# Two-layer attention and feed-forward kernel on one core: banks of the last wide products, products without a reader in TensorE's waits, and an earlier load of the exponential's table

## The reference, cut to what matters

```python
x = x + xattn0(layernorm(x), ctx, ctx)      # 16 heads of 16, softmax attention, Wq Wk Wv Wo
x = x + ffn0(layernorm(x))                  # 256 -> 1024 -> 256: layernorm, 8-bit levels of the activations, ternary weights, exact gelu, layernorm, levels
x = x + xattn1(layernorm(x), ctx, ctx)      # 8 heads of 32, mLSTM form: see below
x = x + ffn1(layernorm(x))                  # base product plus gated low-rank part: see below

# xattn1, over sequences of 128 tokens
pre = 15 * tanh((concat(q, k, v) @ ifgate_w.T + b) / 15)
i_pre, f_pre = pre[..., :8], pre[..., 8:]
log_d = cumsum(log_sigmoid(f_pre)) differences + i_pre, causal;  m = rowmax(log_d)
h = (q k^T / sqrt(32) * exp(log_d - m)) v / (max(|row sum|, exp(-m)) + 5e-5)
out = h / rms(h) * (1 + outnorm_w)

# ffn1: 8 experts of rank 16
gate = softmax(xt @ gate_w.T)
out = xt @ weight.T + (1 / 16) * sum over e of gate_e * (xt @ U_e.T) @ V_e.T
```

## Time and profile before

| | us |
|---|---|
| median of three runs | 413.37 |
| the profiled execution | 413.97 |
| its span (first to last instruction) | 412.3 |
| TensorE busy | 334.4 (81%) |
| VectorE busy | 305.8 (74%) |
| ScalarE busy | 264.3 (64%) |
| gates: last gates' rows turned to first log_d | 289.2 to 297.6 |
| drain: end of the last values' product to the end | 386.3 to 412.3 |

### The profile page before, as it was taken

One profiled execution on the slowest core, in us unless ns is written; L12 is line 12 of the kernel. 1 busy time (PEld: TensorE's weight loads), 2 busy tenths in 40 slices (PEclk: granted clock), 3 DMA queues, 4 the chain that ended last, 5 costly groups with the idle time before them and its releaser, 6 DMA issues.

```text
span 412.3 us, 9147 instructions
## 1 busy us (share of the span) xinstructions
PE 334.4 (81%) x3086; PEld 236.6 (57%) x3093; DVE 305.8 (74%) x1025; ACT 264.3 (64%) x567; POOL 183.8 (45%) x207
## 2 busy tenths in 40 slices
PE   2989789998999999724667778779488999999774
PEld 1777567776777767402445545456265666666431
DVE  2799736877889888676998999984447877788641
ACT  1466445476455455626789889876578888888520
POOL 1213401122122564239998989962015455544520
PEclk9999999999999999955999999989689999999966
DMA  7799998979634510000000000000002122212000
GB/s 239 211 291 264 262 249 221 234 177 227 134 85 115 123 22 2 1 0 0 2 1 2 0 2 1 2 0 2 0 14 40 40 41 53 52 46 46 16 25 25
DMA packets 43869, 33.68 MB, mean 82 GB/s; under 512 B 19888, under 2 KB 39728, under 8 KB 43696
## 3 DMA queue, kind: packets, MB, share of 16 engines
q1 hardware_dynamic: 43824, 33.11, 32.7%
HBM read 24.71 MB, written 8.39 MB: 80 GB/s over the span
## 4 chain that ended last, share of the span: by engine, by line
PE 57%; DVE 18%; issue 13%; ACT 8%; POOL 3%; DMA 1%; SPq 0%; DVEq 0%; ACTq 0%; POOLq 0%
PE PS L1461 6%; PE PS L1157 5%; PE PS L1238 5%; PE PS L1227 4%; DVE sm L741 4%; PE PS L1296 4%; PE PS L1218 4%; PE PS L1217 4%; PE PS L1451 4%; PE PS L1257 3%; PE PS L1446 3%; PE PS L1424 3%; ACT pT L991 2%; DVE sm L713 2%; PE PS L1400 2%
## 5 line engine op out<-in xcount | busy, mean ns | idle before, releaser
L991 ACT ACTIVATE pT<-PS 128x512 f32<-128x512 f32 x64 | 36.5, 596 | 48.2 <-PE PS L1218 47.9
L606 DVE TENSOR_REDUCE negm<-PS 128x4 bf16<-128x512 f32 x64 | 42.3, 684 | 13.0 <-PE PS L1227 12.8
L435 POOL TENSOR_TENSOR sm<-sm,mhalf 128x1 f32<-128x1 f32 x16 | 11.3, 708 | 81.1 <-DVE sm L638 81.1
L451 POOL TENSOR_TENSOR kst<-kst,rows 128x1024 f32<-128x1024 f32 x16 | 37.7, 2354 | 6.4 <-ACT kst L1059 6.3
L1103 ACT ACTIVATE lnT<-PS,Atok 128x128 f32<-128x128 f32 x128 | 36.5, 369 | 4.3 <-PE PS L1402 2.7
L1336 PE MATMUL PS<-identf,w2f 128*128 128x128 f32 x128 | 19.2, 298 | 21.0 <-ACT w2f L1048 20.8
L1218 PE MATMUL PS<-identb,negm 128*128 128x128 bf16 x256 | 34.9, 220 | 0.0
L465 POOL TENSOR_TENSOR kst<-kst,rows 128x1024 f32<-128x1024 f32 x14 | 33.1, 2366 | 0.0
L1238 PE MATMUL PS<-pT,vx 128*32 128x128 f32 x512 | 27.0, 285 | 5.2 <-ACT pT L991 5.2
L1336 PEld LDWEIGHTS PS<-identf,w2f 128*128 128x128 f32 x128 | 15.1, 151 | 25.5 <-ACT w2f L1048 20.2
L1461 PE MATMUL PS<-wd,xT 128*128 128x392 f32 x64 | 28.0, 565 | 1.8 <-DVE rest L885 1.8
(11 more groups left out here) (220 smaller groups left out, 975.6 us busy)
## 6 DMA issues: line engine op xcount, KB each, us to landing
scr_q<-qpart SPq DMA_DIRECT2D x8, 384.0 KB, 3.4
scr_k<-kpart SPq DMA_DIRECT2D x8, 384.0 KB, 4.5
X<-in_x SPq DMA_DIRECT2D x8, 256.0 KB, 4.6
CTXT<-in_ctxT SPq DMA_DIRECT2D x8, 256.0 KB, 4.8
vx<-in_ctx SPq DMA_DIRECT2D x16, 128.0 KB, 3.1
out<-rest SPq DMA_DIRECT2D x16, 128.0 KB, 1.7
rows<-in_rows SPq DMA_DIRECT2D x1, 1544.0 KB, 8.4
qst<-scr_q SPq DMA_DIRECT2D x8, 192.0 KB, 4.5
```

What stands on the lines that cost most here:

```text
L451: gp.tensor_tensor(n2[q.slot], n2[q.slot], ln2g, ALU.mult).then_inc(b_g2, 1)
L606: v.tensor_reduce(negm[f.slot % 2][:, 4 * hg:4 * hg + 4], PS[:, 2 + hg % 2, :].rearrange("p (h k) -> p h k", h=4), AX_X, ALU.max, negate=T ...
L991: s.activation(pT[:, hg, :], PS[:, hg % 2, :], ACT.Exp, scale=float(DH0) ** -0.5).then_inc(a_e, 1)
```

## The change

Four things, in the code's order.

- `wide_bank`: batches 0 to 12 keep bank 7 for the wide product; batches 13, 14 and 15 get banks 2, 3 and 4. Those products no longer wait for the output of the batch before (`d_o`), but for the last attention weights (`c_sm`, 32), which read these banks.
- VectorE's output step is a function `finish`; for batches 12 to 15 it comes at the end of the turn instead of ahead of the update of X.
- `keep_busy(bank, count)`: products of `identb` with `maskb`, 512 bfloat16 columns each, which nobody reads. Three come after the last turned gates, eight after L1367, two after L1370, three after L1373, and three after each of the last three wide products.
- ScalarE loads the table set with the exponential after turn 18 of the feed-forward.

```diff
--- before.py
+++ after.py
@@ -265,6 +265,10 @@
         d_c2 = sem("d_gate_chain"); d_g = sem("d_gated_ready"); d_gt = sem("d_gated_transposed")
         d_gT = sem("d_gatedT_ready"); d_l = sem("d_lora_done"); d_o = sem("d_out_ready")
         d_st = [sem(f"d_stored{i}") for i in range(2)]
+
+        def wide_bank(b):
+
+            return 7 if b < NB - 3 else b - (NB - 3) + 2
 
         block = ctx.enter_context(nc.Block())
 
@@ -855,13 +859,13 @@
 
                     k2.start(d)
                     dve.wait_ge(d_m, d.b + 1)
-                    v.tensor_reduce(ngm[:], PS[:, 7, D + ER:NM], AX_X, ALU.max, negate=True).then_inc(d_mx, 1)
+                    v.tensor_reduce(ngm[:], PS[:, wide_bank(d.b), D + ER:NM], AX_X, ALU.max, negate=True).then_inc(d_mx, 1)
                     dve.wait_ge(d_e, d.b + 1)
                     d_inv = k2.mark(v.reciprocal(ginv[:], esum[:]))
                     done(dve, d_gt, d, 0)
                     dve.wait_ge(d_c2, d_inv)
                     v.scalar_tensor_tensor(out=gt[:].rearrange("p (e r) -> p e r", e=E),
-                                           in0=PS[:, 7, D:D + ER].rearrange("p (e r) -> p e r", e=E),
+                                           in0=PS[:, wide_bank(d.b), D:D + ER].rearrange("p (e r) -> p e r", e=E),
                                            scalar=ginv[:], in1=eD[:].unsqueeze(2).to_broadcast([128, E, R]),
                                            op0=ALU.mult, op1=ALU.mult).then_inc(d_g, 1)
                     k2.end()
@@ -877,12 +881,15 @@
                     dve.wait_ge(c_rr, c.b + 1)
                     v.tensor_tensor(hv[c.slot % 2], hv[c.slot % 2],
                                     rr[c.slot % 2][:].unsqueeze(2).to_broadcast([128, H1, DH1]), ALU.mult).then_inc(c_hd, 1)
-                if d:
+                def finish():
                     dve.wait_ge(d_l, d.b + 1)
                     if d.b >= 2:
 
                         dve.wait_ge(d_st[d.slot % 2], d.b // 2 * 16)
-                    v.tensor_tensor(outb[d.slot % 2], PS[:, 7, 0:D], X[:, d.b, :], ALU.add).then_inc(d_o, 1)
+                    v.tensor_tensor(outb[d.slot % 2], PS[:, wide_bank(d.b), 0:D], X[:, d.b, :], ALU.add).then_inc(d_o, 1)
+
+                if d and d.b < NB - 4:
+                    finish()
                 if c:
                     dve.wait_ge(c_hd, c.b + 1)
                     v.tensor_tensor(X[:, c.b, :], hd[c.slot % 2][:], X[:, c.b, :], ALU.add).then_inc(c_x, 1)
@@ -928,6 +935,8 @@
                     v.scalar_tensor_tensor(out=ms[b.slot % 2][:], in0=den[:, :, 0], scalar=1.0 / DH1, in1=den[:, :, 3],
                                            op0=ALU.mult, op1=ALU.add).then_inc(c_ms, 1)
                     cc.end()
+                if d and d.b >= NB - 4:
+                    finish()
 
             pipeline(dve, NB, 4, 6, turn_cd)
 
@@ -1074,6 +1083,9 @@
             turn_a(*peeled(NB + 3, NB, 4, 5))
             for tau in range(4, NB + 8):
                 turn_b(tau, *peeled(tau, NB, 4, 9))
+                if tau == NB + 2:
+
+                    s.preload_act_table_set("exp_and_others")
 
 
             act.wait_ge(g_tp, 1)
@@ -1106,7 +1118,7 @@
                 if d:
                     act.wait_ge(d_mx, d.b + 1)
                     done(act, d_g, d, 0)
-                    s.activation(eD[:], PS[:, 7, D + ER:NM], ACT.Exp, bias=ngm[:], accum_out=esum[:]).then_inc(d_e, 1)
+                    s.activation(eD[:], PS[:, wide_bank(d.b), D + ER:NM], ACT.Exp, bias=ngm[:], accum_out=esum[:]).then_inc(d_e, 1)
                 if b:
                     act.wait_ge(c_t4, b.b + 1)
 
@@ -1360,17 +1372,26 @@
                 turn_b(*peeled(tau, NB, 4, 9))
 
 
+            def keep_busy(bank, count):
+
+                for _ in range(count):
+                    t.matmul(PS[:, bank, :], identb[:], maskb[:].unsqueeze(1).to_broadcast([128, 4, 128]), start=True, stop=True)
+
             turned(NB - 1).then_inc(g_tp, 1)
+            keep_busy(4, 3)
             If = Ig[:].rearrange("p b h -> p (b h)"); spf = spg[:].rearrange("p b h -> p (b h)")
             pe.wait_ge(g_I, 1)
 
             t.matmul(PS[:, 1, 0:128], If, identf[:], start=True, stop=False)
+            keep_busy(4, 8)
             pe.wait_ge(g_pre, 1)
             t.matmul(PS[:, 1, 0:128], spf, upper[:], start=False, stop=True).then_inc(g_pe, 1)
             t.matmul(PS[:, 2, 0:128], upper[:], spf, start=True, stop=True).then_inc(g_pe, 1)
+            keep_busy(4, 2)
 
             pe.wait_ge(g, 6)
             t.transpose(PS[:, 3, 0:128], MT[:], identf[:]).then_inc(g_tp, 1)
+            keep_busy(4, 3)
 
             def place(q, bank, at):
                 for k in range(PARTS):
@@ -1443,7 +1464,7 @@
                     log_d(0)
                 if d:
                     pe.wait_ge(d_gT, d.b + 1)
-                    t.matmul(PS[:, 7, 0:D], gtT[:], wlv[:], start=False, stop=True, skip_group_check=True).then_inc(d_l, 1)
+                    t.matmul(PS[:, wide_bank(d.b), 0:D], gtT[:], wlv[:], start=False, stop=True, skip_group_check=True).then_inc(d_l, 1)
                 if a:
                     pe.wait_ge(c_ld[a.slot % 2], 16 * (a.b // 2 + 1))
                     pe.wait_ge(c_sm, a.b * 2 + 2)
@@ -1456,10 +1477,17 @@
                     log_d(1)
                 if e:
                     pe.wait_ge(d_xT, e.b + 1)
-                    done(pe, d_o, e, 0)
+                    if e.b < NB - 3:
+                        done(pe, d_o, e, 0)
+                    else:
+
+                        pe.wait_ge(c_sm, 2 * NB)
                     for kc in range(KC):
-                        last = t.matmul(PS[:, 7, 0:NM], xT[:, kc, :], wd[:, kc, :], start=(kc == 0), stop=(kc == KC - 1))
+                        last = t.matmul(PS[:, wide_bank(e.b), 0:NM], xT[:, kc, :], wd[:, kc, :],
+                                        start=(kc == 0), stop=(kc == KC - 1))
                     last.then_inc(d_m, 1)
+                    if e.b >= NB - 3:
+                        keep_busy(5, 3)
 
             pipeline(pe, NB, 4, 6, turn_cd)
```

## The result

The changed kernel takes 407.01 us in the median of four runs (406.27 to 407.31), the kernel before 413.48 beside it: a ratio of 0.984, 95% interval [0.980, 0.987]. The forecast was 406.7, range 404.6 to 410.2. On a second chip the same kernel had 406.73 us against 414.44, 0.982 [0.980, 0.984]. The profiled execution took 406.27 us, span 404.6 against 412.3.

The account below looks back on a forecast made before the run. The prediction took strings of dependent steps at the gates and in the drain, with TensorE at half clock, as the bound; +0.9 - 1.28 - 1.8 - 5.1 = -7.3 from 413.97 gave 406.7 us, range 404.6 to 410.2.

Parts of the forecast that it names:

- The early load, +0.9: Feed-forward: the table load on ScalarE ahead of batch 14's h2T delays what follows by 0.9 us.
- The removed load, -1.28: Gates: the table load between tangent and exponential goes, so the exponential starts 1.28 us earlier.
- The gates, -1.8: Gates: unread products hold TensorE's clock at full, so dependent steps shorten by 1.8 us together.
- The drain, -5.1: Last turns: earlier wide products, moved output step and full clock end the drain at 404.5 instead of 409.64, -5.1 us.
- The other way of counting: Drain: second split of the same gain, clock 4.6 us, order 1.8, less 1.3 taken back.
- the two late turns: Drain, batches 14 and 15: ScalarE and VectorE come late, so these turns are longer and take back 1.3 us.
- That the clock falls in the drain: Rival, drain: the clock falls as before, costing 3.0 us, so about 409.8 us; chance 0.14.
- The load did not come back: Rival, gates: the exponential asks for a table again, so the move only adds 0.9, 408.0 us; chance 0.05.
- Products in front of real work: Rival, gates and drain: unread products starting at half clock delay real ones by 2.8 and 1.1 us; chance 0.03.
- that rival: Gates and drain: half clock when unread products start, so they delay real products, 417.9 us; chance 0.03.
- The full price: Rival, gates and drain: half of 24.5 us at half clock, 12.3 us, comes back, about 401 us; chance 0.04.

Follow-up runs that it names:

- e4: Changed kernel without the early table load, which stands between tangent and exponential again: 407.79 us, ratio 0.985 to the kernel before.
- e5: The changed kernel again, unaltered, beside other runs on the same chip: 406.73 us, ratio 0.982 to the kernel before.
- e9: Kernel before with only the own banks and the moved output step, no unread products, no early load: 410.24 us, ratio 0.990.
- e7: Changed kernel with the table load after turn 20 instead of 18: 406.89 us, ratio 0.983 to the kernel before.
- e1: Changed kernel without the sixteen unread products at the gates: 409.00 us, ratio 0.987 to the kernel before.
- e10: Changed kernel with sixteen unread products instead of eight at the gates' long wait: 408.64 us, ratio 0.987 to the kernel before.
- e11: Changed kernel with four unread products instead of eight at the gates' long wait: 407.03 us, ratio 0.982 to the kernel before.
- e3: Changed kernel with bank 7 for all wide products, the wait for the output, and the output step at its old place: 410.92 us, ratio 0.992.
- e6: Changed kernel with only VectorE's output step back ahead of the update of X in the last four turns: 408.93 us, ratio 0.987.

## Why the prediction was right, and where its working was not

**The early load, +0.9.** It was +0.83 (e4) and, against the profile before, +0.68 (24.17 against 23.49). In all three of these profiles the clock was at half for some time after 271. Of those in which it wasn't, e5 has 24.17 and e9, without the load, 23.26: +0.91. The mechanism was right; e7 shows the better place.

**The removed load, -1.28.** 4.69 to 3.41: -1.28.

**The gates, -1.8.** From L1388 to the first values' product 8.57 became 6.91, -1.66. The steps: 0.79 to 0.49, placing 0.50 to 0.34, log_d to the first exponential 1.08 to 0.65, and from there to the values' product 3.81 to 3.04, where 2.93 was forecast. e1 shows that the unread products carry it (1.68), e10 that sixteen delay the next real product, and e11 that four gave the same way as eight.

**The drain, -5.1.** 23.31 became 17.95, -5.36. The earlier start of batch 13's wide product was forecast at -0.6 and measured -0.77. The three turns behind it were forecast at 4.84, 4.56 and 4.1, and measured 4.83, 4.40 and 4.22, together 13.45 against 13.5. This reckoning, step by step over nd, had the mechanism right.

**The other way of counting was wrong.** "The clock gives ... 4.6 together; the order gives 3 x 0.61 = 1.8; the two late turns take back 1.3": the sum is the same, its split is not. It rests on the sentence that in both places each step that becomes shorter moves the end, "with no other work beside them", and on charging the late normed rows to the new order. The old turn had them too, and later: X's update stood behind the output step, so the ring over X took 5.62 us at full clock, and a wide product at half, 1.5 us longer, mostly ran beside it (0.64 us of it reach the turn in e3, nothing in e6). An estimate from the table: at full clock throughout, the old order would take 5.27 + 5.62 + 5.62 + 4.29 = 20.8 us (e3's turns, its slow one put at 5.62). Then the falls cost the kernel before 2.5 us, not 4.6, and the order gives 2.85, not 0.5. The measured differences have falls of the clock on one side or both and give the order more and the products less. The unread products take 23.31 to 21.44 on the old order, 1.9 us, and 19.48 or 19.22 to 17.95 on the new one, 1.3 to 1.5. The order takes 23.31 to 19.48, 3.8 us, without products, and 3.5 with them. A stall behind two waits was priced by one of them; the total came right since both went.

**The rivals.** That the clock falls in the drain was priced at 3.0 us for three falls; in the profiles without products one fall came, in the last turn, at 1.3 to 1.5. The load did not come back: one stands ahead of h2T, none between tangent and exponential. Products in front of real work cost 1.3 us in e10 and some tenths in e4, never 2.8; and the 417.9 us of that rival leave out what the order gives. The full price by the Trainium skill's formula (TensorE: Matmul & The Clock Gate, Terms), 12.3 us, is not borne out here, the measurement decides: the half-clock stretches in gates and drain are gone, and full clock gave 1.7 us in the one and 1.3 to 2.5 in the other. Most of those stretches was waiting, or TensorE's work beside a longer chain.

**The total.** 0.68 - 1.28 - 1.66 - 5.36 = -7.6 in the profiles, and 7.7 in their times; in the medians it is 6.5, since the profiled execution before was 0.5 us above its median and the changed one 0.7 below. Which stretches of the unprofiled executions make this 1.2 us is not known.

## What to carry to other kernels

Before pricing a stall by the wait that the profile names, follow the ring once around: with the first wait gone, which chain closes the turn, and was it there before? Here, with own banks, moving one VectorE instruction behind the update that others need gave 2.0 us; the three banks gave 1.5, a fall of the clock included. Products that nobody reads held TensorE's clock through the gates' waits in nine of ten profiles, and without them it fell in all three. In the drain they are no guarantee: with them the clock held in eight profiles and fell in the two with turns of 5.6 us (e3, e6). Count them so that they end before the awaited operand comes: eight too many cost 1.34 us. A table load belongs where ScalarE is idle, there and right behind, for about as long as the load: at e7's place ScalarE had been idle for 0.98 us in the kernel before, and again for 0.80 behind the next norm, and the load cost nothing; at the changed kernel's place it had been 0.43, and the load cost 0.7 to 0.9.

## What was not expected of the hardware

The clock also fell in the feed-forward, at other times in other executions of like code, and what a fall costs depends on where it lands. Measured from the third gelu to the last, which takes 79.81 us where it holds: with half clock from 204.53 to 211.36 it took 79.84 (e5), with half clock from 210.12 to 216.94 81.53 (e7). e9 and e10 fell at nearly the same place as e7 and took 81.55 and 81.53. So two falls of the same length cost 0.03 and 1.7 us. These 1.7 us are part of the scatter between runs of one kernel, and no kernel here changes it; how the rest comes about no run shows.
